# A two-layer transformer and state-space kernel: where the first pair's keys, queries and row maxima are handled, and how the running sums are stored

## The reference

```python
q = (x @ Wq).reshape(b, t, 2 * H, HD).transpose(0, 2, 1, 3) * scaling
k = (x @ Wk).reshape(b, t, 2 * H, HD).transpose(0, 2, 1, 3)
v = (x @ Wv).reshape(b, t, H, 2 * HD).transpose(0, 2, 1, 3)
scores = jnp.einsum('bhqd,bhkd->bhqk', q, k)
causal = jnp.triu(jnp.full((t, t), -jnp.inf, dtype=jnp.float32), 1)
aw = jax.nn.softmax((scores + causal).astype(jnp.float32), axis=-1)
lam = jnp.exp(jnp.sum(lq1 * lk1)) - jnp.exp(jnp.sum(lq2 * lk2)) + LAMBDA_INIT
aw = aw[:, :, 0] - lam * aw[:, :, 1]
attn = jnp.einsum('bhqk,bhkd->bhqd', aw, v)
```

## Time and profile before

| | |
|---|---|
| median of three executions | 3575.68 us (3574.21 to 3576.49) |
| the profiled execution | 3574.93 us, span 3572.9 us |
| TensorE busy | 3372.2 us, 94% |
| VectorE busy | 2682.4 us, 75% |
| ScalarE busy | 2108.8 us, 59% |
| POOL busy | 881.3 us, 25% |
| granted TensorE clock, mean | 0.975 |
| DMA | 529.34 MB, mean 148 GB/s |

### The profile page before, as it was taken

How to read it: one execution, slowest core, us unless ns; L and a number is a source line. 1 busy time by engine, 2 the same in 40 slices (tenths; PEclk the granted TensorE clock), 3 DMA queues, 4 the chain that set the end, 5 groups by cost and what they waited for, 6 DMA issues and landing times. The chain is left out here.

```text
span 3572.9 us, 58326 instructions
## 1 busy us (share of the span) xinstructions
PE 3372.2 (94%) x20672; PEld 2379.9 (67%) x20672; DVE 2682.4 (75%) x5220; ACT 2108.8 (59%) x3372; POOL 881.3 (25%) x821
## 2 busy tenths in 40 slices
PE   8889999999999888986999999999999999979998
PEld 6644444444444476765777777777777777758886
DVE  3567777777777484565999989999999899964444
ACT  3146666656666733433777777777777777753332
POOL 0022222222222300001344434443444343420000
PEclk9989999999999998997999999999999999989999
DMA  7433343443442311226666766677666766640100
GB/s 229 77 86 87 103 106 91 107 90 90 108 90 78 121 42 32 86 101 230 230 218 222 261 235 227 223 259 242 231 220 235 249 230 226 220 145 27 36 12 24
DMA packets 264128, 529.34 MB, mean 148 GB/s; under 512 B 32544, under 2 KB 55200, under 8 KB 260768
## 3 DMA queue, kind: packets, MB, share of 16 engines
q1 hardware_dynamic: 263840, 525.62, 46.9%
HBM read 429.55 MB, written 95.42 MB: 147 GB/s over the span
## 5 line engine op out<-in xcount | busy, mean ns | idle before, releaser
L527 ACT ACTIVATE probs<-prob_scores 128x1024 f32<-128x1024 f32 (+3 forms) x640 | 572.5, 896 | 381.5 <-PE prob_scores L457 373.6
L477 PE MATMUL times_v<-probs,VS 128*64 128x256 f32 (+2 forms) x4608 | 612.8, 382 | 15.1 <-ACT outT L561 12.9
L583 DVE TENSOR_REDUCE part_max<-ring 128x1 f32<-128x512 f32 x720 | 463.1, 685 | 115.5 <-PE ring L449 113.8
L49 PE MATMUL sc_pip<-sc_xh,sc_wl 128*128 128x512 f32 x1024 | 456.0, 445 | 26.3 <-DMA sc_xl<-x_low 19.2
L1651 POOL TENSOR_TENSOR sc_xdd<-sc_xdt,sc_small 128x512 f32<-128x512 f32 x128 | 245.6, 1919 | 845.9 <-DVE sc_xdt L1860 845.9
L477 PEld LDWEIGHTS times_v<-probs,VS 128*64 128x64 f32 x4608 | 279.9, 136 | 255.0 <-issue 163.1
L51 PE MATMUL sc_pip<-sc_xh,sc_wh 128*128 128x512 f32 x1024 | 405.0, 396 | 0.0
L50 PE MATMUL sc_pip<-sc_xl,sc_wh 128*128 128x512 f32 x1024 | 403.8, 394 | 0.0
L1785 ACT ACTIVATE sc_M<-sc_later,sc_small 128x128 f32<-128x128 f32 x1024 | 311.8, 390 | 0.0
L1851 DVE SCALAR_TENSOR_TENSOR sc_ca<-sc_xr,sc_chan,sc_ca 128x512 f32<-128x512 f32 x384 | 290.9, 758 | 13.6
L457 PE MATMUL prob_scores<-QS,KS 50*128 50x512 f32 (+3 forms) x1280 | 299.0, 464 | 2.0 <-ACT probs L527 2.0
(11 more groups left out here) (336 smaller groups left out, 7168.0 us busy)
## 6 DMA issues: line engine op xcount, KB each, us to landing
sc_wh<-scan_W_high SPq DMA_DIRECT2D x256, 256.0 KB, 2.8
sc_wl<-scan_W_low SPq DMA_DIRECT2D x256, 256.0 KB, 3.4
sc_later<-scan_acum SPq DMA_DIRECT2D x128, 512.0 KB, 4.8
sc_ce<-scan_expa SPq DMA_DIRECT2D x128, 512.0 KB, 5.2
sc_woh<-scan_Wo_high SPq DMA_DIRECT2D x128, 256.0 KB, 3.9
sc_wol<-scan_Wo_low SPq DMA_DIRECT2D x128, 256.0 KB, 4.8
w_raw<-in_Wg SPq DMA_DIRECT2D x64, 256.0 KB, 2.8
scan_W_high<-w_hi SPq DMA_DIRECT2D x64, 256.0 KB, 2.0
```

What stands on the lines that cost most here:

```text
L49: pe.matmul(out, ll, rh, start=start, stop=False)
L477: mm = pe.matmul(po[MV * s:MV * (s + 1), CHUNK - w + n * h:CHUNK - w + (n + 1) * h], VS[p % 2][:, j, :], PT[u % NPT][:, s, n * h:(n + 1) * ...
L527: act.activation(PT[u % NPT][:, :, 0:w], pb[u % 2][:, :, 0:w], ACT.Exp).then_inc(exped, 1)
L583: dve.tensor_reduce(to, slot(n)[:, 0:w], AX.X, ALU.max).then_inc(emptied, 1)
```

## The change

**First pair's loads.** `load_pair` becomes `load_queries` and `load_keys`. The keys of pair 0 are loaded behind the stores of n = K_DONE + 1 = 29, that is the second piece of Q of the last chunk, the queries ahead of the stores of n = 31. The keys and queries of pair 1 follow the last stores. Row maxima start after V tile SKIP = 1 and end after V tile LAST = 13.

**Maxima and lambda.** Pair 0's split, turn, copy and row stores are moved into stage qkv: the split at the end of VectorE's list, the turn between V tiles 14 and 15. Lambda is also computed there. In stage attention the seven early tiles of pair 1 are gone; its 40 tiles are spread over the steps 0 to 32 of pair 0. POOL's memsets of the probabilities and of outT are left out, with the waits on them; VS and V are staged first.

**Running sums.** They are stored by one DMA for each of the two tables and chunk, in a DRAM layout with all heads of a chunk in one row; the scan loads its group's part of that row. The clearing of the state is moved to POOL.

```diff
+def load_queries(sp, QS, QD, pair, loaded):
...
+            sp.dma_start(QS[at:at + HD, :].bitcast(F32), QD[r // 2, pair * VD + s * HD:pair * VD + (s + 1) * HD, :]).then_inc(loaded, 16)
...
+def load_keys(sp, KS, KD, pair, loaded):
...
+            sp.dma_start(KS[at:at + HD, :].bitcast(F32), KD[r % 2, pair * VD + s * HD:pair * VD + (s + 1) * HD, :]).then_inc(loaded, 16)
...
+def split_row_maxima(dve, nm, mp, part, made, high, low, n):
+    dve.tensor_reduce(nm[:, :, :].rearrange("p s i -> p i s"), part[:, :, :, :], AX.X, ALU.max, negate=True).then_inc(made, 1)
+    dve.wait_ge(made, n + 1)
+    flat = nm[:, :, :].rearrange("p s i -> p (s i)")
+    dve.tensor_copy(mp[:, 0:2 * TT], flat).then_inc(high, 1)
+    dve.wait_ge(high, n + 1)
+    dve.tensor_tensor(mp[:, 2 * TT:4 * TT], flat, mp[:, 0:2 * TT].bitcast(F32), ALU.subtract).then_inc(low, 1)
+def load_max_rows(sp, Q, mT, loaded):
+    for k in range(2):
+        for s in range(2):
+            at = (2 * k + s) * TT
+            row = 64 * s + 3 * HD + k
+            sp.dma_start(Q[row:row + 1, :].bitcast(F32), mT[at:at + TT, :].bitcast(F32)).then_inc(loaded, 16)
...
-    SKIP = 2
-    first_tile = [max(n - SKIP, 0) * len(tiles) // (TT - SKIP) for n in range(TT + 1)]
+    SKIP, LAST = 1, TT - 3
+    first_tile = [min(max(n - SKIP, 0), LAST + 1 - SKIP) * len(tiles) // (LAST + 1 - SKIP) for n in range(TT + 1)]
...
+                sp.wait_ge(w_low, 1)
+                for n, v in enumerate(lams):
+                    sp.dma_start(lv[:, n, :], v.partition_broadcast(P)).then_inc(lam_in, 16)
                 for n, (w, m, c) in enumerate(outs):
+                    if n == len(outs) - 1:
+                        sp.wait_ge(out[0], 32 * (len(outs) // NS))
+                        sp.wait_ge(prod, len(outs))
+                        load_queries(sp, g.QS[0], QD, 0, loaded[0])
                     sp.wait_ge(low, n + 1)
                     for part, s in enumerate((sh, sl)):
                         sp.dma_start((QD, KD)[w][part, m * P:(m + 1) * P, c * CHUNK:(c + 1) * CHUNK],
                                      s[:, n % NS, :].bitcast(F32)).then_inc(out[n % NS], 16)
+                    if n == K_DONE + 1:
+                        sp.wait_ge(out[0], 32 * ((K_DONE - EK) // NS + 1))
+                        sp.wait_ge(ready, 4)
+                        load_keys(sp, g.KS[0], KD, 0, loaded[0])
+                sp.wait_ge(ready, 5)
+                load_keys(sp, g.KS[1], KD, 1, loaded[1])
+                load_queries(sp, g.QS[1], QD, 1, loaded[1])
+                sp.wait_ge(max_copied, 1)
+                sp.wait_ge(loaded[0], 16 * 12)
+                load_max_rows(sp, g.QS[0], mT, max_in)
                 for i in range(NS):
                     sp.wait_ge(out[i], 32 * (len(outs) // NS))
-                sp.wait_ge(ready, 5)
-                sp.wait_ge(prod, len(outs))
-                for b in range(2):
-                    load_pair(sp, g.QS[b], g.KS[b], QD, KD, b, loaded[b])
-                for b in range(2):
-                    sp.wait_ge(loaded[b], 16 * 12)
+                sp.wait_ge(loaded[1], 16 * 12)
+                sp.wait_ge(max_in, 64)
...
+                act.wait_ge(lam_sum, 2)
+                act.activation(le[:, 2:4], le[:, 0:2], ACT.Exp).then_inc(lam_exp, 1)
...
+                dve.wait_ge(emptied, 2 * len(tiles))
+                dve.wait_ge(out[0], 32 * (len(outs) // NS))
+                split_row_maxima(dve, nm, mp, g.part, max_all, max_high, max_low, 0)
+                dve.wait_ge(max_turned, 1)
+                dve.tensor_copy(mT, ps[NV][:, 0:P]).then_inc(max_copied, 1)
...
+                    if i == LAST + 1:
+
+                        pe.wait_ge(max_low, 1)
+                        pe.transpose(ps[NV][:, 0:P], mp.bitcast(F32), g.ident[:, :]).then_inc(max_turned, 1)
...
-        q, t = (p + 2, u - START) if u >= START else (p + 1, EARLY + u)
-        return [(q, t)] if q < PAIRS else []
-    place = {("turn", 0): 0}
-    for t in range(EARLY):
-        for s in range(2):
-            place["max", 1, t, s] = len(place)
+        if u >= START:
+            of = [(p + 2, u - START)]
+        elif p:
+            of = [(p + 1, EARLY + u)]
+        else:
+            of = [(1, t) for t in range(u * NM // START, (u + 1) * NM // START)]
+        return [(q, t) for q, t in of if q < PAIRS]
+    place = {}
...
-                pool.memset(mp[:, :].bitcast(F32), 0.0).then_inc(setup, 1)
+                def stage_v(p):
+                    pool.tensor_copy(VS[p % 2][:, :, 0:VD], g.V[:, :, p * VD:(p + 1) * VD]).then_inc(v_staged, 1)
+                for b in range(2):
+                    pool.memset(VS[b][:, :, :], 0.0).then_inc(setup, 1)
+                pool.wait_ge(setup, 2)
+                for b in range(2):
+                    pool.memset(VS[b][:, :, VD], 1.0).then_inc(setup, 1)
+                stage_v(0)
                 for b in range(2, NQK):
                     pool.memset(KS[b][:, :].bitcast(F32), 1.0).then_inc(setup, 1)
-                for b in range(2):
-                    pool.memset(VS[b][:, :, :], 0.0).then_inc(setup, 1)
-                pool.wait_ge(setup, 4)
-                for b in range(2):
-                    pool.memset(VS[b][:, :, VD], 1.0).then_inc(setup, 1)
-                for b in range(NPT):
-                    pool.memset(PT[b][:, :, :], 0.0).then_inc(pt_free, 1)
-                pool.memset(OT[0][:, :], 0.0).then_inc(po_free, 1)
+                pool.memset(mp[:, :].bitcast(F32), 0.0).then_inc(mp_clear, 1)
                 for p in range(PAIRS):
 
-                    pool.tensor_copy(VS[p % 2][:, :, 0:VD], g.V[:, :, p * VD:(p + 1) * VD]).then_inc(v_staged, 1)
+                    if p:
+                        stage_v(p)
...
-                sp.wait_ge(emptied, place["turn", 0] + 1)
-                max_rows(sp, 0)
+                sp.wait_ge(setup, 4 + NQK - 2)
...
                         pe.wait_ge(v_staged, p + 1)
+                        if p == 0:
+                            pe.wait_ge(setup, 4)
...
-                pe.wait_ge(setup, 6)
-                turn_maxima(0)
-                for t in range(EARLY):
-                    max_scores(1, t)
-                pe.wait_ge(max_in[0], 64)
...
-                            for grp in range(GROUPS):
-                                sp.dma_start(D[name][grp * TT + QT * c:grp * TT + QT * (c + 1), :].rearrange("c (h l) -> h c l", l=CL),
-                                             src[grp * GH:(grp + 1) * GH, :].rearrange("h (c l) -> h c l", l=CL)).then_inc(out, 16)
+                            sp.dma_start(D[name][QT * c:QT * (c + 1), :].rearrange("c (h l) -> h c l", l=CL),
+                                         src[:, :].rearrange("h (c l) -> h c l", l=CL)).then_inc(out, 16)
...
+                def by_head(t, name):
+                    return D[name][chunk_of(t), group_of(t) * GH * CL:(group_of(t) + 1) * GH * CL].partition_broadcast(P)
...
+                pool.memset(st[:, 0, :], 0.0).then_inc(cleared, 1)
+                pool.memset(st[:, 1:, :], 0.0).then_inc(cleared, 1)
...
-                for buf in (st[:, :, :], sd[:, :]):
-                    dve.memset(buf, 0.0).then_inc(cleared, 1)
```

120 lines of the change are left out of this document (54 added, 66 removed).

## The result

The changed kernel takes 3557.39 us (median of 5 runs, 3556.82 to 3561.66) against 3575.68 before, of 5 runs too: a ratio of 0.9952 with a 95% interval of 0.9938 to 0.9967, some 18 us. On a second chip it took 3559.15 us against 3574.95, ratio 0.9955 [0.9942, 0.9967]. The profiled execution took 3559.05 with a span of 3557.1, which is 15.8 less than the span before.

A forecast was written before the change was run, and what follows sets the result against it. TensorE, busy for most of the span, was taken as the bound, with time to gain where it stands still or is slow. 7.2 us from pair 0 and 1.4 from the sums made 8.6: 3567.1 us, range 3561 to 3573.

The forecast's parts named there:

- The loads' landing: Stage qkv, pair 0: loads and two stores at 1.11 us each, in order, last at 119.6; wait 9.5 us.
- The rival on overlap: Stores pass beside loads, 2.2 us earlier: 3564.9; double steps stalling less too: down to 3559.7; chance 0.15 together.
- The rest of the stage: Stage qkv after the first maxima: last group at 166.8, stage end at 178.2; only 2.05 us gained.
- The start of attention: First product with V at 183.3 instead of 198.11, held by POOL's list; 14.8 us gained, 2.05 included.
- The double steps: Pair 0 of attention: seven second tiles wait for a ring bank; 7.6 us lost, bounds 2.4 and 11.1.
- The clock at the second joint: From stage qkv into attention: rival that the clock holds, saving 3.3 us at half clock: 3563.8; chance 0.17.
- The running sums: End of the experts stage: two stores for sixteen, last store out at 1616.8; 1.4 us gained, bounds 0 and 1.5.
- The sum: Whole kernel: 7.2 us by the end of pair 0 plus 1.4 from the running sums, 8.6 us gained.
- The scan rival: In the scan: 128 steps each wait 0.2 us for their sums, 25.6 us, making 3592.7; chance 0.04.

The follow-up runs named there:

- e7: The changed kernel with pair 0's twelve loads behind all stores of Q, still keys first, then queries; 3566.75 us, ratio 0.9981 to the kernel before.
- e8: The changed kernel with two memsets of POOL (third key buffer, maxima) moved behind the fourth mask of pair 0; 3560.80 us, ratio 0.9963 to the kernel before.
- e5: The changed kernel with the second tile of each double step of pair 0 behind the product with V; 3556.48 us, ratio 0.9945 to the kernel before.
- e13: The changed kernel with seven early tiles back at attention's start and matmuls of no use at both joints; 3560.35 us, ratio 0.9957 to the kernel before.
- e6: The kernel before with only the running sums' new stores and layout; 3572.70 us, ratio 0.9994.
- e10: The changed kernel with matmuls of no use filling TensorE's waits at both joints; 3557.56 us, ratio 0.9955 to the kernel before.

## Why the prediction was wrong, point by point

**The loads' landing: the step that failed.** "Two stores, at a load's 1.11 for want of a nearer row", and six and six loads at 1.11 each, made 119.6. They landed at 0.78, with the stores beside them in a stretch of 228 GB/s, and the first maxima came at 115.03, 4.6 us earlier. All of it is pace. The first key landed at 105.2 as forecast: the whole stage ran 0.9 us earlier (the stores of the earlier trace rows at 97.88 are at 96.99, and between 96.57 and 98.03 in the sixteen traces, so that this is no work of the change), but that key took 4.6 us to land. From there to the last query were 9.7 us for 14.4: ten steps of 0.78 for 1.11 are 3.3 of the difference, and 1.9 for 3.3 between the last key and the first query, where the two stores stand, the rest. The wait was 5.83 and not 9.5. The queue was rightly taken as the limit, its rate wrongly as fixed and its landings wrongly as one behind the other: 1.11 came from loads alone, by turns, with 119 GB/s, and the second store landed behind a query issued after it. The rival on overlap had the right direction and a price of 2.2 us; it counted the stores as free but the loads still at 1.11. e7 shows the loads themselves faster than 1.11 (0.84), and their last landing, behind the stores, 5.0 us later than among them. Why the pace moves stays open.

**The rest of the stage: right.** From the first maxima to the last group at 162.55 were 47.5 us for 47.2, although 5.8 us of work ran at half clock there for 4.1 before, which no term held. The transpose waited 0.92 for about 1.5, and attention's first instruction came at 173.76, 11.2 behind that group for 11.4.

**The start of attention: right.** From the stage's start to the first product with V were 4.9 us for 5.1, ended by POOL's mask as said, and e8 shows that POOL's list was what held it, by 1.65.

**The double steps: right in size.** Seven waits, 5.1 us in all, for some 5.2 of stall in the forecast's 7.6. From the first product with V to the next copy of V the changed kernel takes 70.59 us and the kernel before 64.13: 6.46 more. With 3.1 us less of half clock behind that product, worth 1.5, this is 8.0 for the forecast 7.6.

**The clock at the second joint: a rival that came half true.** The clock did fall, but came back earlier, 3.5 us after the first product with V and not 6.6; the forecast took the old length over without a reason, and nothing here explains the new one, so these 1.5 us are luck. e7 and e5 to e13 show that this stretch is 0 to 20 us of slow work from one kernel to the next, so a forecast had to carry it as several us either way; mine gave it 3.3 us at a chance of 0.17.

**The running sums: right mechanism, too small.** 1.49 us by the earlier issue, forecast 1.4; another 1.14 because the last store landed sooner, which no term held. e6 gives both alone.

**The sum.** Pair 0 ended 12.98 us earlier and not 7.2: 4.6 from the loads, 1.5 from the clock, less 0.4 by dearer double steps. The lead shrank by 0.7 between the last pair and the last chunk's sums, these gave 2.63 for 1.4, and the scan and the last network another 0.8, both well inside the scatter behind the second copy of V. The scan rival, slower by waiting for its sums, did not occur.

## What to carry to other kernels

A landing pace read from a row of like transfers is no constant of the queue: before a sum rests on it, look whether the row had only loads or only stores in it, and hold the range open to twice the bytes per second when the change mixes them. Whoever shortens a wait of TensorE by a few microseconds should count the slow work behind it as a term with a wide range of its own; in these traces it differed by more than the edits did. Edits of a few microseconds are better compared at an event right behind them than by the time of the whole kernel. A last store is worth moving out from behind a row of others twice, once for its issue and once for its landing.

## What the runs showed of the hardware

Loads into 16 partitions moved 119 to 160 GB/s with the DMA engines busy throughout; their order, and whether they stood right behind the stores, each gave about 10 and both together 41. Among stores the same queue moved 228 over the 11 us of the changed kernel, and 289 over the six shown of e10; there a load landed before a store issued ahead of it. TensorE's clock fell once behind 3.74 us of work in 4 and stayed at half for 20 us of unbroken work (e13), while in the changed kernel it was back 3.5 us after the first product with V. Matmuls of no use in a wait of 5.8 us kept the clock up at the first joint in three kernels of three, worth 2.6 us, and at the second in one of three. Behind the second copy of V single executions of the same instructions still differ by 8 us.
